# Decoder layer on one core: the experts' down products as four 512-column and four 256-column matmuls a tile, the right half gated by ScalarE and added by GpSimd

## The reference

```python
h = relu(einsum('edi,bsi->bsed', proj_in, x))      # 256 -> 512, per expert
o = einsum('eid,bsed->bsei', proj_out, h)          # 512 -> 256, per expert: the "down" product
gate = einsum('bks,bkse->bse', weights, onehot)
x = layernorm(x + einsum('bsei,bse->bsi', o, gate))
```

## Time and profile before

| | before |
|---|---|
| median of 3 runs | 806.56 us |
| the profiled execution, its own time | 806.47 us |
| its span | 804.6 us |
| TensorE busy | 788.1 us, 98% |
| TensorE weight loads busy | 686.8 us, 85% |
| VectorE / ScalarE / GpSimd busy | 459.6 / 307.2 / 103.5 us |

### The profile page before, as it was taken

How to read it: one execution, slowest core, us unless ns; L and a number is a source line. 1 busy time by engine, 2 the same in 40 slices (tenths; PEclk the granted TensorE clock), 3 DMA queues, 4 the chain that set the end, 5 groups by cost and what they waited for, 6 DMA issues and landing times.

```text
span 804.6 us, 12925 instructions
## 1 busy us (share of the span) xinstructions
PE 788.1 (98%) x4382; PEld 686.8 (85%) x4382; DVE 459.6 (57%) x1126; ACT 307.2 (38%) x555; POOL 103.5 (13%) x102
## 2 busy tenths in 40 slices
PE   8999889999999999999999999999999999999996
PEld 6888779999999989999999988888888888888885
DVE  4788768876577757777666654225522552245124
ACT  6788542223232323223232245433543354326331
POOL 3776130002020201002020000000000000000000
PEclk9999999999999999999999999999999999999998
DMA  9500000003113131221211000000000000000000
GB/s 336 201 1 0 2 2 1 1 1 105 54 53 106 40 93 53 78 76 42 92 53 53 1 7 1 1 1 26 0 0 0 20 7 0 0 14 13 1 1 29
DMA packets 15747, 31.46 MB, mean 39 GB/s; under 512 B 1616, under 2 KB 6224, under 8 KB 15440
## 3 DMA queue, kind: packets, MB, share of 16 engines
q1 hardware_dynamic: 15264, 30.04, 11.6%
q10 hardware_dynamic: 432, 0.79, 0.3%
HBM read 28.72 MB, written 2.10 MB: 38 GB/s over the span
## 4 chain that ended last, share of the span: by engine, by line
PE 94%; DVE 3%; issue 1%; DMA 1%; ACT 1%; POOL 0%; SPq 0%; DVEq 0%
PE bank L778 31%; PE bank L969 29%; PE bank L893 23%; PE bank L806 7%; PE bank L984 3%; DMA wp_lo_f<-in_wproj 1%; PE bank L858 0%; DVE b_tok L1034 0%; DVE hx_lo L1194 0%; DVE sp L1026 0%; PE bank L913 0%; PE bank L912 0%; DVE x_tok L1332 0%; PE bank L865 0%; PE bank L864 0%
## 5 line engine op out<-in xcount | busy, mean ns | idle before, releaser
L684 ACT ACTIVATE hx_hi<-bank 128x512 fp32r<-128x512 f32 x128 | 76.7, 599 | 263.2 <-PE bank L778 263.1
L893 PE MATMUL bank<-wx_hi,hx_lo 128*128 128x256 f32 x512 | 144.9, 283 | 0.0
L893 PE MATMUL bank<-wx_lo_r,hx_hi 128*128 128x256 f32 x512 | 144.8, 283 | 0.0
L893 PE MATMUL bank<-wx_hi,hx_hi 128*128 128x256 f32 x512 | 144.3, 282 | 0.0
L1194 DVE SCALAR_TENSOR_TENSOR hx_lo<-bank,hx_hi 128x512 fp32r<-128x512 f32 x128 | 88.4, 690 | 86.3 <-ACT hx_hi L684 85.8
L778 PE MATMUL bank<-xT_hi,wx_hi 128*128 128x512 f32 x256 | 101.7, 397 | 2.3 <-DVE xT_lo L1189 1.3
L893 PEld LDWEIGHTS bank<-wx_hi,hx_hi 128*128 128x128 f32 x512 | 97.7, 191 | 5.4
L893 PEld LDWEIGHTS bank<-wx_lo_r,hx_hi 128*128 128x128 f32 x512 | 97.7, 191 | 4.8
L778 PE MATMUL bank<-xT_lo,wx_hi 128*128 128x512 f32 x256 | 101.1, 395 | 0.0
L969 PE MATMUL bank<-ha_hi_r,wf_hi_r 128*128 128x512 f32 x256 | 100.0, 391 | 0.0
L969 PE MATMUL bank<-hb_hi_r,wf_hi_r 128*128 128x512 f32 x256 | 99.9, 390 | 0.0
(11 more groups left out here) (154 smaller groups left out, 1376.3 us busy)
## 6 DMA issues: line engine op xcount, KB each, us to landing
stage<-in_wffn SPq DMA_DIRECT2D x44, 256.0 KB, 2.6
wx_lo_f<-in_wx SPq DMA_DIRECT2D x16, 512.0 KB, 4.0
x_tok<-in_x SPq DMA_DIRECT2D x1, 2048.0 KB, 11.8
out<-x_tok SPq DMA_DIRECT2D x16, 128.0 KB, 1.7
xs_lo_f<-in_xT SPq DMA_DIRECT2D x3, 512.0 KB, 5.9
wp_lo_f<-in_wproj SPq DMA_DIRECT2D x2, 512.0 KB, 7.6
ctx_sb<-in_ctx SPq DMA_DIRECT2D x1, 1024.0 KB, 8.0
itok_sb<-in_itok SPq DMA_DIRECT2D x1, 1024.0 KB, 9.9
```

The lines of the kernel that those rows point to most:

```text
L684: act.activation(hx_hi[:, place, c], bank[b][:, :], ACT.Relu).then_inc(s_relu_ok, 1)
L893: mm = pe.matmul(bank[2 + j % 2][:, 0:D], x_, w_, start=(c == 0 and i == 0), stop=(c == XC - 1 and i == 2))
```

## The change

- **The down product.** The two halves of the weights now lie in one tensor wx_both, so that hx_hi times [w_hi | w_lo] is one matmul of 512 columns (left half of a bank: hi·hi, right half: hi·lo), and hx_lo times w_hi is one of 256 columns into the left half. A token tile takes four of each in place of twelve of 256. The bank of tile j is one of four (2, 3, 6, 7) rather than one of two.
- **The right half.** VectorE gates and adds the left half as before. ScalarE multiplies the right half by the gate into a buffer `right` (two slots); it does so one step later, after its next relu. GpSimd adds the buffer to the row.
- **Order on GpSimd.** GpSimd now walks through all units and tiles. The quarters of wx_lo are placed between its additions: those of expert 2p+1 behind the additions of tiles 0 and 2 in u = 2 and in u = 3, those of expert 2p+2 behind the same tiles in u = 6 and 7.
- **Order on the others.** ScalarE's part of the second norm comes at c = 3 of the last unit. VectorE's halves_x comes ahead of `low` at c = 2. Transposes of later groups share banks 4 and 5, so that ScalarE and VectorE wait for both tiles of a bank. TensorE's down waits also for s_right_ok (the tile four before in the same bank), VectorE's `gated` for s_row_ok.
- **The flag.** A one-element matmul of wide_col with itself replaces partition_all_reduce.

```diff
+        DBANK = [bank[i] for i in (2, 3, 6, 7)]
+
+        def x_bank(g, j):
+
+            if isinstance(g, int) and g == 0:
+                return bank[4 + j][:, 0:D]
+            return bank[4 + j // 2][:, j % 2 * D:j % 2 * D + D]
...
+            def right_added(unit, g, j):
+                pool.wait_ge(s_right_ok, unit * J + j + 5)
+                row = x_tok[:, g * J + j]
+                pool.tensor_tensor(row, right[:, j % 2], row, ALU.add).then_inc(s_row_ok, 1)
+
+            def expert_low(e, n, parts=range(4)):
+                for c in parts:
                     pool.wait_ge(s_wxhi_ok, n * 4 + c + 1)
...
+            def step(g, further, last):
+                for j in range(J):
+                    right_added(g * 2, g, j)
+                    if last and j == 0:
+                        expert_low(0, 2, (0, 1))
+                for j in range(J):
+                    if further and j == 2:
+                        root(g + 2)
+                    right_added(g * 2 + 1, g, j)
+                    if last and j == 0:
+                        expert_low(0, 2, (2, 3))
...
             def pair(p, last):
-                expert_low(1, p * 2 + 1)
-                if not last:
-                    expert_low(0, p * 2 + 2)
-            pairs_of_experts(pool, pair)
...
-            pool.wait_ge(s_wide_c, 1)
-            pool.partition_all_reduce(wide_all[:, :], wide_col[:, :], P, RMAX).then_inc(s_wide_a, 1)
+                for u in range(8):
+                    for j in range(J):
+                        right_added(p * 8 + u, u % G, j)
+                        if u in (2, 3) and j % 2 == 0:
+                            expert_low(1, p * 2 + 1, ((u - 2) * 2 + j // 2,))
+                        if u in (6, 7) and j % 2 == 0 and not last:
+                            expert_low(0, p * 2 + 2, ((u - 6) * 2 + j // 2,))
+                    if u == 5 and last:
+                        ln_rstd(s_f_ve, s_f_rstd, 1)
...
+            def right_half(unit, g, j, expert):
+
+                act.wait_ge(s_gated_ok, unit * J + j + 5)
+                act.wait_ge(s_row_ok, unit * J + j + 3)
+                gate = gates[:, bass.ds(g * J + j, 1), bass.ds(expert, 1)].rearrange("p b e -> p (b e)")
+                act.activation(right[:, j % 2], DBANK[j][:, D:2 * D], ACT.Copy, scale=gate).then_inc(s_right_ok, 1)
...
             def pair(p, last):
                 for u in range(8):
-                    if u < 7 or not last:
-                        for c in range(XC):
+                    for c in range(XC):
+                        if u < 7 or not last:
                             relu(p * 8 + u + 1, (u + 1) % 2, c, c % 2)
+                        if u == 7 and last and c == 3:
+                            keep(0)
+                            norm2_T(0, True)
+
+                        if c > 0:
+                            right_half(p * 8 + u, u % G, c - 1, p * 2 + u // G)
+                        else:
+                            right_half(p * 8 + u - 1, (u - 1) % G, J - 1, p * 2 + (u - 1) // G)
...
+                pe.wait_ge(s_right_ok, unit * J + j + 1)
                 a = slice(j * S, j * S + S)
                 for c in range(XC):
                     if j == 0:
                         pe.wait_ge(s_hlo_ok, unit * XC + c + 1 + 2)
-                    for i, (x_, w_) in enumerate(three(hx_hi[:, place, c, a], hx_lo[:, place, c, a], wo_h[:, c], wo_l[:, c])):
-                        mm = pe.matmul(bank[2 + j % 2][:, 0:D], x_, w_, start=(c == 0 and i == 0), stop=(c == XC - 1 and i == 2))
+                    if c > 0:
+                        pe.matmul(DBANK[j][:, 0:D], hx_lo[:, place, c, a], wo_h[:, c], start=False, stop=False)
+                    mm = pe.matmul(DBANK[j][:, :].rearrange("p (h d) -> p h d", h=2), hx_hi[:, place, c, a], wo_hl[:, :, c],
+                                   start=(c == 0), stop=(c == XC - 1))
+                    if c == 0:
+                        pe.matmul(DBANK[j][:, 0:D], hx_lo[:, place, c, a], wo_h[:, c], start=False, stop=False)
                 mm.then_inc(s_down_mm, 1)
...
+                        if u == 6 and last and c == 2:
+
+                            pe.wait_ge(s_wide_c, 1)
+                            pe.matmul(bank[5][0:1, 0:1], wide_col[:, :], wide_col[:, :], start=True, stop=True).then_inc(s_wide_mm, 1)
                         if u == 7 and last and c == 2:
+                            pe.wait_ge(s_wide_f, 1)
                             norm2_T(0)
...
+                        if c == 2 and front:
+                            halves_x(g + 1)
                         low(g * 2 + 1, 1, c, c % 2)
                         if c == 0 and front:
                             norm_apply(lambda j: group_row(g + 1, j), lambda j: group_row(g + 1, j), g + 1, s_rstd_ok, s_xn_ok)
-                        if c == 2 and front:
-                            halves_x(g + 1)
...
-                dve.wait_ge(s_gated_ok, B * E + 2)
+                dve.wait_ge(s_gated_ok, B * E + 4)
+                dve.wait_ge(s_row_ok, B * E + 4)
```

More of the change, by code:

```diff
@@ L85, in decoder_kernel @@
         stage = small("stage", [2, PIECE])
+        right = small("right", [2, D])
         assert base[0] <= 229344
@@ L121, in decoder_kernel @@
         w_scratch = at("w_scratch", o_ha, [B, D])
-        wx_hi = at_r("wx_hi", o_hb, [2, WX])
-        wx_lo, wx_raw = both("wx_lo", o_hb + 2 * WX * 4, [2, WX])
+        wx_both = at_r("wx_both", o_hb, [2, 2, WX])
+        wx_hi, wx_lo = wx_both[:, 0], wx_both[:, 1]
+        wx_raw = at("wx_raw", o_hb + 2 * WX * 4, [2, WX])
         hx_hi = at_r("hx_hi", o_ha, [2, XC, N])
@@ L226, in decoder_kernel @@
         s_gated_ok = sem("gated_ok")
+        s_right_ok = sem("right_ok")
+        s_row_ok = sem("row_ok")
         s_wxhi_ok = sem("wxhi_ok")
@@ L295, in decoder_kernel, with norm_bank @@
         UBANK = [bank[i] for i in (1, 2, 6, 7)]
+        DBANK = [bank[i] for i in (2, 3, 6, 7)]
[3 more added lines that the diff above has]
+            return bank[4 + j // 2][:, j % 2 * D:j % 2 * D + D]
+        def norm_bank(n0, j):
+            return bank[(0, 1, 4, 5)[j] if isinstance(n0, int) and n0 == 0 else 4 + j][:, 0:D]
         def row_products_dma(sp_, rows, done):
@@ L509, in _, with ln_rstd @@
             groups_behind(pool, project)
-            def expert_low(e, n):
-                for c in range(4):
+            def ln_rstd(sem_in, sem_out, n, a=slice(0, J)):
+                pool.wait_ge(sem_in, n)
+                pool.tensor_tensor(rstd[:, a], var_eps[:, a], neghalf[:, a], ALU.pow).then_inc(sem_out, 1)
+            def right_added(unit, g, j):
[4 more added lines that the diff above has]
+                for c in parts:
                     pool.wait_ge(s_wxhi_ok, n * 4 + c + 1)
@@ L526, in _ @@
             expert_low(1, 1)
[L528 to L533, removed]
-            def pair(p, last):
-                expert_low(1, p * 2 + 1)
-                if not last:
-                    expert_low(0, p * 2 + 2)
-            pairs_of_experts(pool, pair)
[L542 to L545, removed]
-            pool.wait_ge(s_wide_c, 1)
-            pool.partition_all_reduce(wide_all[:, :], wide_col[:, :], P, RMAX).then_inc(s_wide_a, 1)
+            def step(g, further, last):
[9 more added lines that the diff above has]
+                        expert_low(0, 2, (2, 3))
+            root(1)
+            for g in range(G):
+                step(g, g < G - 2, g == G - 1)
+            def pair(p, last):
+                for u in range(8):
[7 more added lines that the diff above has]
+                        ln_rstd(s_f_ve, s_f_rstd, 1)
+            for p in range(1, E // 2):
+                pair(p, p == E // 2 - 1)
             pool.wait_ge(s_wide_f, 1)
@@ L695, in step @@
                     relu(g * 2 + 2, 0, c, c % 2)
+                    if c > 0:
+                        right_half(g * 2 + 1, g, c - 1, 1)
+                    else:
+                        right_half(g * 2, g, J - 1, 0)
                     if c == 1 and not front:
                         expert_high(0, 2, (2, 3))
+            act.sem_inc(s_right_ok, 4)
             halves_x(0)
@@ L700, in _ @@
                 relu(0, 0, c, 4 + c)
-            steps(act, step)
+            for g in range(G):
+                step(g, g < G - 1)
             def keep(n0):
@@ L724, in pair @@
                         expert_high(0, p * 2 + 2)
-                    if u == 7 and last:
-                        keep(0)
-                        norm2_T(0, True)
             pairs_of_experts(act, pair)
+            right_half(E * G - 1, G - 1, J - 1, E - 1)
             act.wait_ge(s_wide_f, 1)
@@ L883, in down @@
                 wo_h = wx_hi[:, e, OUT].rearrange("p (c d) -> p c d", c=XC)
-                wo_l = wx_lo[:, e, OUT].rearrange("p (c d) -> p c d", c=XC)
+                wo_hl = wx_both[:, :, e, OUT].rearrange("p h (c d) -> p h c d", c=XC)
                 if j == 0:
@@ L941, in ffn @@
                     if m == 1:
```

(14 more changed lines are left out.)

37 lines of the change are left out of this document (23 added, 14 removed).

## The result

The changed kernel takes 815.09 us (median of 4 runs, 814.9 to 817.13) against 806.52; the ratio is 1.0112, 95% interval 1.0098 to 1.0126. Forecast was 811.5, range 804.5 to 818.5.

The account below looks back on a forecast made before the run. TensorE's issue was taken to bound the kernel, with no slack: 806.5 less 8.8 us for the new down plus 13.8 us of waits for wx_lo gives 811.5 us; range 804.5 to 818.5, 8 times in 10.

Parts of the forecast that it names:

- What bounds it: Expert pairs: TensorE is busy all the time without waits, so each nanosecond of its issue counts in full, 128 times.
- The order of GpSimd, first wait: First up of a new expert: TensorE stands 1.97 us for quarter 1 of wx_lo, five times, plus 0.1 restart each.
- T: Moment in u = 2, c = 3 when TensorE passes from the up to the down of tile 2.
- Second wait: Down of tile 0, one unit later: TensorE stands 0.60 us for quarter 3 of wx_lo, plus 0.1 for the restart.
- The gain of the new down: Down and following up: 69 ns less in 124 steps, 53 ns less in four downs, about 8.8 us gained.
- 256s after a 512 at 113.5 (three): In the new down, three of four 256-column matmuls follow a 512 and cost 113.5 ns each, free of surcharge.
- three after a 256 at 230: In the new down, three 512-column matmuls that follow a 256 cost 230 ns each.
- The upper bound of the waits: TensorE's waits for wx_lo with the longest rows, additions up to 1.25 and quarters up to 1.48 us: 16.5 us.
- no stall, 797.7: Rival: the wx_lo stalls don't come, only the down's gain does; 797.7 us, between 794 and 804; 13 in 100.
- VectorE behind GpSimd: Rival: GpSimd's additions stretch VectorE's SBUF operations, ten units at about 0.5 us on top; 816.5 us; 9 in 100.
- Two runs as dear as two matmuls: Rival: in the down, a 512 with two runs costs as two 256s; 821.6 us; 8 in 100.
- Costs set to nothing: Waits on s_right_ok, shared transpose banks, the flag's matmul and the feed-forward's start were each taken to cost nothing.

Follow-up runs that it names:

- experiment 3: Kernel before, only GpSimd's wx_lo quarters 1 and 3 made to wait for the relu of c = 3, as late as in the changed kernel: 812.02 us, ratio 1.0062.
- experiment 1: Changed kernel with an expert's four wx_lo quarters behind the additions of tiles 0 to 3 of u = 2 (and u = 6): 801.24 us, ratio 0.9935.
- Experiment 2: Changed kernel with only quarter 1 of wx_lo moved one tile forward, behind tile 1 of u = 2 and of u = 6: 804.19 us.
- Experiment 6: Kernel of experiment 1 with a tile's four 512-column matmuls first and its four of 256 behind them: 801.25 us, step 2767 ns.
- experiment 4: Changed kernel with unread identity matmuls ahead of each first up of a new expert: 821.84 us with 16, 813.83 us (ratio 1.0090) with 8.
- experiment 8: Kernel of experiment 1 timed again, 800.73 us; with VectorE's loop over pairs written out, 799.90; with ScalarE's and TensorE's too, 800.01.
- experiment 7: Kernel of experiment 1 without GpSimd's 128 additions, semaphore steps kept: 800.61 us.
- experiment 5: Kernel of experiment 1 with the 512-column matmul's moving operand as one run of 512 columns, not two of 256: 801.15 us, step 2767 ns.

## Why the prediction was right, point by point

- **What bounds it**: TensorE's issue, with nothing to give a wait back. Right. Each wait on TensorE came through to the time, in the changed kernel and in experiment 3.
- **The order of GpSimd, first wait**: forecast 1.97 us five times; measured 1.92. Right in its chain and its size: TensorE started 3.33 us behind T (235.73 to 239.06), not 3.35. The right half was longer than taken, 0.47 us and not 0.39; the addition and the quarter together were shorter by 0.1. Experiments 1 to 3 show that it is the cause.
- **Second wait**: forecast 0.60 us and 0.1 for the restart; measured, with the restart, 0.59 twice, 0.69, 0.86 and 0.88, together 3.6 against 3.5. Right; why two are longer stays open. Experiment 2 prices it at 3.0 us.
- **The gain of the new down**: forecast 69 ns a step and 8.8 us, measured 53 and 6.7. The direction is right, the term too large by 2.1 us. The step of the working that failed is "256s after a 512 at 113.5 (three)" with its 512s, "three after a 256 at 230": the 256 was near 113.5 once and 117 to 120 after, and those 512s took 233 to 241. So the down, taken at 1377 ns, is 1407, and the up, taken at 1374, is 1360: all of its surcharge went, not half. Experiment 6 shows that what a 256 saves is charged to a neighbour; the difference between 96 and 43 ns for eight 256s fewer is 6.6 ns each, the 120 - 113.4 of the earlier trace rows. Counting 256s, not neighbours, would have given the 53.
- **The lower clock**: missed. The working priced a stand by its length and a restart of 0.1 us. In the profiled run two of five stands brought 1.67 us each on top; with the stand filled, in experiment 4, it doesn't come. From 811.5 to the median of 815.1: the gain was 2.1 us too large, the waits and restarts came to 13.5 and not 13.8, which makes 813.3; the 1.8 us left agree with what experiment 4 gives back, but no trace shows that they are the clock.
- **The number**: the two misses add up and don't cancel, so that the time fell inside the range by no luck.
- **The upper bound of the waits**: 16.5 us doesn't follow from the rows that it names. An addition of 1.25 and a quarter of 1.48 us in each of the ten waits give 20.7, and 828.5 in place of 824.3 for the outer end. The forecast and the range of 804.5 to 818.5 don't use it.
- **The rivals**: no stall, 797.7: refuted, though it is near the 799.9 of experiment 8, which removes the stall. VectorE behind GpSimd: as a cost to TensorE refuted by experiment 7 and by TensorE's waits; the additions do stretch VectorE's operations. Two runs as dear as two matmuls: refuted by experiment 5.
- **Costs set to nothing**: the four banks, the wait on s_right_ok, the shared transposes, the flag and the start of the feed-forward (0.6 us of wait for xf_lo before and after). Right; none appears among TensorE's waits.

## What to carry to other kernels

When a helper engine takes on small work that follows the main engine step by step, its whole list is tied to that pace: look for the one long-lead product in the list (here a weight quarter) and place it by when it is wanted, counted back from the instruction that waits, not where the engine has room. On a TensorE that never waits, price a merge of matmuls by how many narrow ones disappear (here 6.6 ns for each one of 256 columns), and look at what the clock does behind a stand of some 2 us.

## What the runs showed of the hardware that was not expected

- Behind a stand of TensorE of 1.9 us the granted clock fell to its lower level in two of five cases of one execution (matmuls of 512 columns 0.43 us apart, not 0.23); behind those of 0.8 to 0.94 us in experiment 3 in none of five. The Trainium skill (TensorE: Matmul & The Clock Gate, HAM oscillation) tells of such a fall for gaps longer than this one; here it came with a shorter one.
- A profile with its clock column at 0.95 throughout and others at 1.00 have the same distances, 227 ns for 512 columns. A mean of 0.947 against 0.994 was no difference in speed.
- A matmul with both operands in plain fp32, 128x128, is two records 0.112 us apart, 0.224 us for the matmul (experiment 4), nearly the 0.227 of 512 columns in float32r.
- At the turn of its hardware loop, in experiment 1, VectorE stood 4.5 us: `low` started at 297.51 though the relu that it reads had ended at 294.16 (293.56 + 0.60). The kernel before has a stand of 4.0 us at the same place, and there the two steps of TensorE behind it were only 0.2 and 0.1 us too long. What the engine does in that time, and why TensorE lost more in experiment 1, is open.

```profile
293.56 0.60 ACT L719 ACTIVATE hx_hi<-bank 128x512 fp32r<-128x512 f32 x1 [1.64 <-PE bank L836]
297.51 0.69 DVE L1264 SCALAR_TENSOR_TENSOR hx_lo<-bank,hx_hi 128x512 fp32r<-128x512 f32 x1 [4.46 <-ACT hx_hi L719]
```
